# Three edits to a two-layer decoder kernel: when an expert batch's last product runs, what the projections of the second cross attention wait for, and who makes a quarter of the ternary weight pieces

## The reference

```python
# L0_ffn: 8 experts as low-rank changes of one base, top 2 of 8 per row
h_e = silu(base_up + lo_up) * (base_gate + lo_gate);  ch = c[:, None] * h_e
mixed_h += ch;  lora_down += 2 * (ch @ down_A[e].T @ down_B[e].T)
out = mixed_h @ w_down.T + lora_down
# L1_xattn: 16 query heads of 128 on 8 key heads, context 256 x 256
out = softmax(q @ k.T / sqrt(128)) @ v @ Wo
# L1_ffn: ternary weights, s = mean(|w|)
wq = round(tanh(w / (s + 1e-8))) * arctanh(s)
```

## Time and profile before

| | |
|---|---|
| median of 3 runs | 3378.43 us (3375.62 to 3384.37) |
| the profiled execution | 3379.68 us, of it a span of 3377.7 us |
| busy in the span | PE 2857.4 us (85%), DVE 2074.5 (61%), ACT 1771.8 (52%), POOL 1409.7 (42%) |
| granted clock of TensorE, mean | 0.947 |

### The profile page before, as it was taken

How to read it: one execution, slowest core, us unless ns; L and a number is a source line. 1 busy time by engine, 2 the same in 40 slices (tenths; PEclk the granted TensorE clock), 3 DMA queues, 4 the chain that set the end, 5 groups by cost and what they waited for, 6 DMA issues and landing times. The chain is left out here.

```text
span 3377.7 us, 64410 instructions
## 1 busy us (share of the span) xinstructions
PE 2857.4 (85%) x24866; PEld 2022.3 (60%) x24866; DVE 2074.5 (61%) x4462; ACT 1771.8 (52%) x3857; POOL 1409.7 (42%) x1537
## 2 busy tenths in 40 slices
PE   3999999947888884999999888878999999975787
PEld 1666666624666663777777666666666677642333
DVE  4667767756777765455555456655555555565886
ACT  3555555546888884233332266654444444454775
POOL 1444444425887881444444434451111112213553
PEclk9999999978999986999999999999999999997899
DMA  4000000010000004000000001002010110031000
GB/s 163 1 1 1 1 1 1 1 66 1 2 2 2 2 2 158 1 7 7 1 1 1 26 30 39 14 1 69 14 32 32 38 38 1 1 100 50 13 13 26
DMA packets 41189, 81.49 MB, mean 24 GB/s; under 512 B 5683, under 2 KB 9781, under 8 KB 40758
## 3 DMA queue, kind: packets, MB, share of 16 engines
q1 hardware_dynamic: 40886, 77.38, 6.8%
HBM read 73.18 MB, written 4.19 MB: 23 GB/s over the span
## 5 line engine op out<-in xcount | busy, mean ns | idle before, releaser
L1072 POOL TENSOR_TENSOR c_pT<-c_prob,c_pT 128x512 f16<-128x512 f32 x256 | 293.3, 1159 | 102.8 <-ACT c_pT L1029 102.2
L1925 POOL TENSOR_TENSOR c_prob<-c_prob,c_inv 128x512 f32<-128x512 f32 x128 | 133.5, 1043 | 310.5 <-DVE c_inv L2149 310.5
L1072 POOL TENSOR_TENSOR a_pT<-a_prob,a_pT 128x384 f16<-128x384 f32 x128 | 120.7, 945 | 189.9 <-ACT a_pT L1029 189.5
L733 DVE SCALAR_TENSOR_TENSOR a_pT<-psT,a_kvh_t,a_pT 128x256 f16<-128x256 f32 (+1 forms) x256 | 94.6, 410 | 169.6 <-ACT a_pT L642 169.6
L1263 ACT ACTIVATE c_prob<-psT 128x512 f32<-128x512 f32 x256 | 156.1, 610 | 69.4 <-PE psT L1194 55.4
L1344 DVE TENSOR_REDUCE c_peak<-psS 128x2 f32<-128x512 f32 x256 | 169.6, 683 | 20.5 <-PE psS L1175 17.2
L444 POOL TENSOR_TENSOR a_q_rot<-a_q_cos,a_q_sin 128x512 f32<-128x512 f32 x64 | 81.1, 1267 | 193.1 <-DVE a_q_sin L752 193.1
L1029 ACT CAST c_pT<-c_prob 128x512 f16<-128x512 f32 x256 | 159.9, 625 | 0.0
L2073 ACT CAST c_pT<-psT 128x512 f16<-128x512 f32 x128 | 74.8, 584 | 140.5 <-PE psT L1937 140.5
L2065 ACT ACTIVATE c_prob<-psS,c_negmax 128x256 f32<-128x256 f32 x256 | 119.2, 474 | 44.5 <-DVE c_negmax L2142 40.8
L463 POOL TENSOR_TENSOR a_prob<-a_prob,a_inv 128x128 f32<-128x128 f32 x128 | 52.4, 409 | 214.3 <-DVE a_inv L726 214.3
(11 more groups left out here) (630 smaller groups left out, 11387.7 us busy)
## 6 DMA issues: line engine op xcount, KB each, us to landing
c_feed<-in_L_ffn_w1T SPq DMA_DIRECT2D x16, 512.0 KB, 3.8
c_feed<-in_L_ffn_w2T SPq DMA_DIRECT2D x16, 512.0 KB, 3.7
f_stage<-in_f_up_gateT SPq DMA_DIRECT2D x16, 352.0 KB, 7.0
x_all<-in_x SPq DMA_DIRECT2D x1, 4096.0 KB, 14.3
a_stage<-in_L_attn_WqT SPq DMA_DIRECT2D x8, 512.0 KB, 7.5
a_stage<-in_L_attn_WoutT SPq DMA_DIRECT2D x8, 512.0 KB, 10.1
a_feed<-in_L_xattn_Wq SPq DMA_DIRECT2D x8, 512.0 KB, 3.7
c_feed<-in_L_xattn_Wo SPq DMA_DIRECT2D x8, 512.0 KB, 3.8
```

The lines of the kernel that those rows point to most:

```text
L733: last = dve.scalar_tensor_tensor(pT[1][:, r, m, m * P:N], T[:, m * N + m * P:(m + 1) * N], kvh_t[:, b % 2, m, H + h:H + h + 1], pT[0][:, ...
L1072: pool.tensor_tensor(pT[1][:, c % NPH, :], prob[:, c % NPX, :], pT[0][:, c % NPH, :], ALU.subtract)\
L1925: pool.tensor_tensor(prob[:, h % NPB, :, :], prob[:, h % NPB, :, :], inv[:, h % NPB, :].rearrange("p (n a) -> p n a", a=1).broadcast_to([P ...
```

## The change

1. `ffn0`: the six `dB` matmuls are taken from the end of a batch on PE and put behind the next batch's router and `wA` products (`finish(b - 1)`); the last batch keeps them at its end. On DVE `add_and_measure` of batch b-1 moves behind `f_picked` of batch b (`measure(b - 1)`), and its `normalize` behind `f_mask`.
2. `xattn1`: projections 2 and 3 wait for `var_ready` of tile 0 and of tile 1, counted up by the last operation of a tile's `add_and_measure` (Y has been read by then), and no longer for both normalised tiles at projection 2.
3. Of the last batch's 16 pieces every fourth, formerly `signs`, is of a new kind, `third`: POOL makes it in two halves of 128x512, three operations each, behind its division of heads 1, 3, 5 and so on. DVE handles piece i-1 instead of piece i in step i. The ring waits for the second half where the old piece is a `third`. POOL waits for the thresholds before the last batch's heads.

```diff
 class Feed:
     def fetch(self, sp, n):
         for i in range(self.fetched, self.fetched + n):
-            if i >= self.ring:
-                sp.wait_ge(self.done, i - self.ring + 1)
+            before = i - self.ring
+            if before >= 0 and self.items[before][0] == "third":
+                sp.wait_ge(self.third_done, 2 * self.thirds[before])
+            elif before >= 0:
+                sp.wait_ge(self.done, before + 1 - self.thirds[before])
...
+    def third(self, pool, h):
+        i = [i for i, item in enumerate(self.items) if item[0] == "third"][h // 2]
+        kind, src, hi, lo = self.items[i]
+        raw, hi = self.staged(i)[:, h % 2, :], hi[:, h % 2, :]
+        m = self.halves[:, h % 2, 0:raw.shape[1]]
+        self.has_landed(pool, i)
+        pool.tensor_scalar(m, raw, self.thr[:, 3 + lo:4 + lo], None, ALU.is_lt).then_inc(self.halved, 1)
+        pool.tensor_scalar(hi, raw, self.thr[:, lo:lo + 1], None, ALU.is_gt).then_inc(self.halved, 1)
+        pool.wait_ge(self.halved, 2 * h + 2)
+        pool.tensor_tensor(hi, hi, m, ALU.subtract).then_inc(self.third_done, 1)
...
 ffn0, PE
+                def finish(b):
+                    after(pe, s.z_parts, b, 1)
+                    for n in range(NT):
+                        at = slice(n * P, (n + 1) * P)
+                        three(pe, Y[n][:, :], zs[0][:, at], zs[1][:, at], dB[0][:, 0, :], dB[1][:, 0, :], False, True)\
+                            .then_inc(s.y_ready.handle, 1)
...
                     last.then_inc(s.a_ready.handle, 1)
+                    if b:
+                        finish(b - 1)
                     base(0)
...
-                    after(pe, s.z_parts, b, 1)
-                    for n in range(NT):
...
+                finish(B - 1)
 ffn0, DVE
                     last.then_inc(s.picked_ready.handle, 1)
+                    if b:
+                        measure(b - 1)
                     after(dve, s.top_turned, b, 1)
...
                         .then_inc(s.mask_ready.handle, 1)
+                    for n in range(NT if b else 0):
+                        normalize(dve, s, b - 1, n, G)
...
-                    for n in range(NT):
-                        add_and_measure(dve, s, b, n, Y[n][:, :], s.y_ready, G, steps)
-                    for n in range(NT):
-                        normalize(dve, s, b, n, G)
 xattn1
-                    fed.append((("sign", "signs")[len(fed) % 2], drams[i][at], G.w12[i][at], i))
+                    fed.append((("sign", "signs", "sign", "third")[len(fed) % 4], drams[i][at], G.w12[i][at], i))
...
+                        if b == B - 1 and h % 2:
+                            feed.third(pool, h // 2)
...
-                        if i == 2:
-                            after(pe, s.x_done, b, 0)
+                        if b and i in (2, 3):
+                            after(pe, s.var_ready, b - 1, i - 1)
...
-                            feed.low(dve, SIGNS[i])
+                            feed.low(dve, SIGNS[i - 1] if i else 0)
```

More of the change, by code:

```diff
@@ L173, in __init__ @@
         self.highs = [sum(k in ("split", "sign") for k, *_ in items[:i + 1]) for i in range(len(items))]
+        self.thirds = [sum(k == "third" for k, *_ in items[:i + 1]) for i in range(len(items))]
+        if self.thirds[-1]:
+            self.third_done, self.halved = sc.sem(f"{name}_third"), sc.sem(f"{name}_halved")
+            self.halves = sc.sb(f"{name}_halves", [P, 2, 512], F16)
     def staged(self, i):
@@ L217, in low @@
                 last = dve.scalar_tensor_tensor(hi, raw, self.thr[:, lo:lo + 1], hi, ALU.is_gt, ALU.mult)
+            elif kind == "third":
+                continue
             else:
@@ L1568, in ffn0 @@
         s.y_ready = sc.counter("y_ready", NT)
-        s.chain = sc.counter("chain", 1 + 2 * NT + 2 + 3 + 3 + NT * LN_STEPS)
+        s.chain = sc.counter("chain", 1 + 2 * NT + 2 + 3 + 3)
+        s.ln_chain = sc.counter("ln_chain", NT * LN_STEPS)
         s.pool_chain = sc.counter("pool_chain", 1 + TH_)
@@ L1700, in _ @@
                             last.then_inc(s.down_done.handle, 1)
-                    after(pe, s.z_parts, b, 1)
-                    for n in range(NT):
-                        at = slice(n * P, (n + 1) * P)
-                        three(pe, Y[n][:, :], zs[0][:, at], zs[1][:, at], dB[0][:, 0, :], dB[1][:, 0, :], False, True)\
-                            .then_inc(s.y_ready.handle, 1)
+                finish(B - 1)
             @block.scalar
@@ L1745, in _, with measure @@
                 x_low(dve, 0, s, xT, G.psS)
+                def measure(b):
+                    steps = Steps(dve, s.ln_chain, b)
+                    for n in range(NT):
+                        add_and_measure(dve, s, b, n, Y[n][:, :], s.y_ready, G, steps)
+                    steps.check()
                 for b in range(B):
@@ L1811, in _ @@
                         .then_inc(s.z_parts.handle, 1)
-                    for n in range(NT):
-                        add_and_measure(dve, s, b, n, Y[n][:, :], s.y_ready, G, steps)
-                    for n in range(NT):
-                        normalize(dve, s, b, n, G)
                     steps.check()
+                measure(B - 1)
+                for n in range(NT):
+                    normalize(dve, s, B - 1, n, G)
 def xattn1(nc, G, W):
@@ L1922, in _ @@
                         see(b + 1)
+                    else:
+                        pool.wait_ge(w_step, 7)
                     for h in range(H):
```

## The result

The changed kernel takes 3367.5 us (median of 7 runs, 3362.37 to 3373.72) where the kernel before takes 3378.43 (7 runs, 3374.16 to 3384.55). The ratio on record is 0.9959, with a 95% interval of 0.9947 to 0.9971: 14 us, or 0.4%, faster; the two medians alone differ by 10.9 us. I had forecast 3349 us and a range of 3338 to 3362; the time lies outside it. The profiled execution has a span of 3368.7 us against 3377.7.

A forecast was written before the change was run, and what follows sets the result against it. PE, busy 85% of the span, was taken as the bound, so its standstills could be won: 3379.7 - 4.4 - 13.6 - 12 = 3349.7 us, stated as 3349 because the runs' median is 1.3 lower; range 3338 to 3362.

The forecast's parts named there:

- It just fits: Second cross attention: projection 4's input from DVE is done at about 2390.5, PE arrives at 2390.60; part 2 gives -13.6 us.
- The rival with projection 4: Projections: DVE's low part comes 1 us later, projection 4 takes over the wait, part 2 gives 7 us; 3356 us, chance 0.05.
- 1.6 won and 1.0 given back: Expert layer, per batch: PE's standstill before dB goes, normalisations lengthen DVE's chain; 11.4 less 7.0, net -4.4 us.
- The whole 1.0 us lands in PE's wait for `f_h`: Expert layer: two normalisations behind the mask delay the first f_h by 1.0 us a batch, 7.0 us back over seven.
- part 1 returns nothing: Rival, expert layer: normalisations push POOL's three operations by as much again, so no gain; 3353 us, chance 0.10.
- the price T: Last batch: time of one half on POOL, 0.85 + 0.85 + 1.16 plus 0.4 for a meeting, 3.3 us; ends 1.7 and 4.4.
- Period = 12.8 + T: Last batch: four heads take a chain of 12.8 us plus the price T, 16.1 against 19.3; three periods give 9.5 us.
- the start: Last batch: the first late division is done at about 2982.2, which gives 1.7 us.
- The end of the batch: Last batch: the last head's exponential is not held by a step of the feed, which gives 1.3 us.
- In 19, which says that T is above 6: Sign for the last batch: four heads taking 19 us would mean the forecast was wrong and the price T above 6.
- the meetings rival: Last batch: DVE's pieces hold POOL for their whole length, T 6.2, period 19.0, gain about 1 us; 3360 us, chance 0.14.
- DVE loses four pieces: Last batch: DVE loses four signs pieces of some 2.0 us and sign leaves the row maximum's path; together part 3's -12 us.

The follow-up runs named there:

- e1: Changed kernel with parts 1 and 3 undone, so only the new waits of projections 2 and 3 differ from the kernel before: 3370.42 us, ratio 0.9961.
- e3: Changed kernel with the expert layer's two normalisations on DVE put ahead of the mask's copy instead of behind it: 3353.97 us, ratio 0.9919.
- e6: Changed kernel with GpSimd's three operations on each half replaced by one memset, fetches and waits kept: 3347.67 us, ratio 0.9898.
- e7: Changed kernel with piece kinds ordered sign, signs, third, sign, so GpSimd's piece is fetched one earlier: ratio 0.9921.
- e10: Changed kernel fetching only 16 of 512 columns of each GpSimd piece, all operations at full size: ratio 0.9933.
- e4: Changed kernel with no pieces on GpSimd, all 16 made as before, DVE's piece still one head later: 3350.62 us, ratio 0.9905.
- e5: Changed kernel with normalisations ahead of the mask's copy and no GpSimd pieces, DVE's piece still one head later: 3340.92 us, ratio 0.9872.
- e9: As e5, but with the piece kinds turned round to signs, sign: 3338.85 us, ratio 0.9875.

## Why the prediction was wrong, by its steps

- **Part 2, right.** "It just fits" held: 14.0 us, no new wait, and e1 shows it alone. The rival with projection 4 did not come.
- **Part 1, the sum of the waits, nearly right.** 1.6 won and 1.0 given back per batch was forecast; measured are 1.8 and 0.86 (12.8 and 6.0 us over seven), and batches of 74.0 against 75.03 where the clock stays up. The 1.6 was read at one boundary, and five of the seven have 1.9.
- **Part 1, the step that failed.** "The whole 1.0 us lands in PE's wait for `f_h`" treats a wait as costing its own length. Here it lengthened one wait from 0.6 to 1.5 us, and behind it the clock fell in about half the batches, at 1.7 us each: in five of seven in the profiled execution, so that the part gave +1.8 us and not -4.4. e3, which shortens the wait and moves nothing on PE, ends that. The rival "part 1 returns nothing" had the right size by luck: its mechanism was GpSimd's pushed operations.
- **Part 1, what I saw and didn't use.** I wrote that DVE idles 2.28 us ahead of the mask and that the sums are ready 2.9 us before it. Both say that the normalisations fit there; that would have been the better change, and its price was in my own rows.
- **Part 3, the step that failed most: the price T.** The part gave 0.5 us and not 12. 3.3 us was the term; measured are 4.3 for the second half of a piece and 5.2 for the first, which is the one in the chain. The comparison was the miss: 1.56 us against my 0.85, next to my upper end of 1.6. I had put it below both rows that I had, the cast of 128x128 scaled fourfold (1.17) and the division (1.04), for a fixed part that no row shows. Between its own ends T was worth 11 us of the forecast.
- **Part 3, the chain.** Period = 12.8 + T was the right form: e6 (T down), e7 and e10 (landing earlier) all shorten it. The constant was 1.0 short: 19.0 - 5.2 = 13.8. Half a us of that is the four transposes at the lower clock behind the long wait (1.11 for 0.60), which I did not count; the rest was not split. T and the constant together make 2.9 us in each of three periods, 8.7 of the 11.5 us that are missing; the start gave 0.9 and not 1.7. The end of the batch, from the last such transposes on, was to be 1.3 us shorter and is 1.1 longer: 15.6 us before (from 3041.84), 16.7 now (from 3034.58), with the lower clock for 6.8 us behind PE's wait and not for 3.4.
- **Part 3, the sign that misled.** "In 19, which says that T is above 6": four heads take 19.0 with T at 5.2. The period of the meetings rival, also 19.0, was hit by luck, since its T was 1.0 too high and the constant 1.0 too low.
- **Part 3, what it was worth to take from DVE.** The forecast took it for granted that DVE must lose work. e4 shows 15.9 us a period with DVE's work unchanged: only the order mattered. I had the two causes in one sentence ("DVE loses four pieces, *and* a sign piece no longer stands between Abs and the next row maximum") and never priced them apart.
- **Meetings of GpSimd and DVE.** The first rival priced them at 3.3 us for a half; they cost 0.9 in the first half (0.5 and 0.4) and nothing in the second. See the rows below. I had also put the division's 0.43 us more at 2974.64 down to line 224; in the timeline it met line 221, which ran from 2974.48 to 2975.21, and line 224 started only behind that. The rival's total, 3360, was nearest to the result, again with another mechanism.
- **Range.** The parts sum to 3348.4, written as 3349. I took each bound into it but not both bad ends together, and no case in which a wait costs more than itself.

## What to carry to other kernels

A wait on PE can cost twice its length where the clock falls behind it, so after an edit look at the granted clock by stretches, not only at the list of waits. Before work is moved to an idle engine, try to move it in time on the engine that has it; an in-order engine with a division due every few microseconds is not idle for a block of 5 us. And when an edit bundles two causes, price each alone, since the cheaper one may be all that is needed.

## What the runs showed of the hardware

- **The clock behind a wait.** With a wait of 0.6 to 0.7 us for `f_h` it never fell in the expert layer (before, e1, e3, e5, e9: 35 batches); with 1.5 to 1.6 us at the same place it did in 23 of 49, and came back after 3.4 us each time. The length alone isn't it: ahead of `dB` the kernel before stood still as long or longer at each of seven boundaries (idle 1.46 us at two, 1.75 at five), and in its last batch PE waited 1.8 us for a division five times between 2993 and 3033 us, and no fall followed any of them. What sets the wait for `f_h` apart was not found, nor why one batch has the fall and the next not: a wait of 1.46 or 1.47 us stands ahead of both, and so does the 1.57 of the second batch, with a fall in three kernels and without in four.
- **GpSimd's comparison** against a scalar of each partition, 128x512, float32 to float16, takes 1.56 us; its subtraction of two float16 tiles takes 1.16, its division of 128x512 (in the code a product with the reciprocal, float32) 1.04 and a memset 0.53. The operation with one tensor to read is the slowest.
- **Meetings lengthen by the overlap.** DVE's operation with a piece and a mask, and GpSimd's comparison, in the changed kernel:

```profile
2988.91 1.28 DVE L233 SCALAR_TENSOR_TENSOR f_wq<-c_feed,thr,c_larger 128x1024 f16<-128x1024 f32 x1
```

```profile
2989.51 2.12 POOL L244 TENSOR_SCALAR c_feed_halves<-c_feed,thr 128x512 f16<-128x512 f32 x1 [1.88 <-DMA c_feed<-in_L_ffn_w2T]
```

  GpSimd's starts 0.68 us ahead of DVE's end and takes 0.55 longer; in e10 DVE's runs from 2981.47 to 2982.75, GpSimd's starts 1.12 ahead of that end and takes 1.00 longer. Whoever starts second stands still for about as long as both would run, so these two engines don't meet at semaphores only. The Trainium skill's page "SBUF — State Buffer", section "SBUF: two separate sides", says the same, that the one that starts first has the shared ports for its whole instruction. I had weighed that rule against "part of an operation" as if they were two cases; the rows are one case, in which the cost is what is left of the first when the second starts. These two meetings agree with it, and so does the one of the earlier trace rows: GpSimd's division ran for 0.87 us more (2974.64 + 1.47 - 2975.24) when DVE's operation started, and that took 0.66 longer.
